# Sharing batch 0's normalisation between two engines, and another order of first loads, in a one-core adaLN block

## The chip, the cores and the metric

The program runs on one core of a Trainium2 chip. The metric is the device time of one execution in microseconds (us). The engines are PE (TensorE, with its weight loads as PEld), DVE (VectorE), ACT (ScalarE), POOL (GpSimd) and SP (SyncE, which here only issues DMAs); "SPq" and "ACTq" are the DMA issues on the queues of SP and ACT.

## What is computed

x is 16 batches of 512 tokens by 128 features, all float32. With h of 128 features:

```python
mod = (silu(c) @ wmod).reshape(16, 6, 1, -1)      # c: [16, 128], wmod: [128, 768]
sa, ca, ga, sb, cb, gb = (mod[:, n] for n in range(6))
ga, gb = sign(g) * max(|g|, 0.25) of each
h = layernorm(x) * (1 + ca) + sa
q = h @ Wq + bq                                    # q, k and v are the same
x = x + ga * (softmax(q @ q.T / sqrt(128)) @ q)    # per batch
h = layernorm(x) * (1 + cb) + sb
# top-1 routing over 8 experts: sigmoid(h @ Wr + br), argmax, its probability as factor
x = x + gb * prob * (gelu(h @ W1[e]) @ W2[e])
```

## The kernel before

A batch is held as a tile of 128 partitions by 4 blocks (j = 0 to 3) of 128 features; a partition holds four consecutive tokens. The kernel has three parts: a head (the modulation from c, and the first batches' start), attention slots (one per batch, each engine with its own hand-written order in which four batches are in work at once), and the expert part (39 tiles of 256 or 128 tokens). In an attention slot k, batch k is scored and mixed, batch k+1 is projected, batch k+2 is normalised, batches k-1 and k-2 are routed. Slots -2 and -1 fill this pipeline.

**The head.** SP issues four loads in this order: `cond` (c, 8 KB, L361), `wmod_sb` (384 KB, L362), x of batch 0 and x of batch 1 (256 KB each, L342). ACT waits for `cond` and computes `cond_e` = exp(-c) (L695), and then issues four small loads on its own queue (Wq, bq, Wr, br; L696 to L699). DVE computes `cond_d`, `cond_s` and `silu` (L879 to L883), then `ln1` of batch 0 (4 statistics L865, 4 aggregates L868) and `variance1` (L874, L875), the copy `silu_t` (L887), and the same of batch 1. POOL turns the variance into `rstd1` by a power (L1376) and then `offset1` (L1379). ACT's `normalize1` writes the four blocks of `xn` (L708).

PE transposes `silu` (L448), and multiplies by `wmod_sb`: four products give shift and scale as columns in the PSUM tile `side[1]` (L452), two give the gate rows in `mixed[1]` (L456). Then `flip_xn` transposes the four blocks of `xn` into `side[1]` (L469). As the columns lie in the same bank, it waits until DVE has copied them out (`s_dve0`, L892 to L895). ACT's `input_t` applies scale and shift and writes `h_t` (L721), PE projects it (`project`, L479), ACT writes `q_t` and `q_hi` (L733, L737), DVE `q_lo` (L919), and PE transposes `q_t` (`flip_v`, L487).

**The gates.** DVE makes `gate_rows` from the two gate products in four instructions (L899 to L904). SP waits for them, stores them to DRAM (L367), waits for the store, and then, in its slots, issues the load of x of batch 2, `load_gate1` of batch 0 (the gate row read back, broadcast to all partitions, L350), x of batch 3, the gate of batch 1, and W1 (2 MB, L375). DVE's `values` needs both the transposes of `flip_v` and this gate:

```python
dve.wait_ge(v_flipped, b.n + 1)
dve.wait_ge(gate1_loaded[b.p], 16 * (b.h + 1))
nc.vector.tensor_tensor(v_sb[:, b.p, :, :], side[1][:]..., gate1[:, b.p, :]..., ALU.mult).then_inc(v_ready, 1)
```

In DVE's order `values` of batch 0 (L928) stands ahead of `find_max` of batch 0, block 0 (L937), whose result the first exponential on ACT needs (L747). In PE's order the scores of batch 0, block 0 (L500 to L502) are followed by `flip_xn` of batch 1, which waits for `v_ready` (the same PSUM bank `side[1]`), and that by the scores of block 1 and `flip_probs` (L512). The later `flip_v`, `values`, `find_max` and `residual` repeat for each batch.

Of the kernel before, what the change touches and what calls it, by code (L numbers as in the profile page):

```python
# [11 lines left out]
ALU = mybir.AluOpType  # L12
# [10 lines left out]
def batch_at(n):  # L23
    return Batch(n, n % 2, n // 2, n % PAYLOADS, n // PAYLOADS, n % X_TILES, n // X_TILES)


def adaln_block(nc, x_in, Wq, bq, Wr, br, W1, W2, c_in, wmod, out):
    B, S, H = x_in.shape
    E, _, F = W1.shape
    J = S // P  # L30
    KF = F // P
# [24 lines left out]
    with ExitStack() as ctx:  # L56
        def sb(name, shape, dt=F32):
            return ctx.enter_context(nc.sbuf_tensor(name, shape, dt))

        def sem(name):  # L60
            return ctx.enter_context(nc.semaphore(name))
# [4 lines left out]
        mixed = [ctx.enter_context(nc.psum_tensor(f"mixed{n}", [P, 512], F32)) for n in range(2)]  # L66
        side = [ctx.enter_context(nc.psum_tensor(f"side{n}", [P, 512], F32)) for n in range(2)]
# [25 lines left out]
        cond = sb("cond", [B, H])  # L93
# [4 lines left out]
        silu_t = sb("silu_t", [P, B])  # L98
        wmod_sb = sb("wmod_sb", [P, 6 * H])
        shift1 = sb("shift1", [P, B])  # L100
        scale1 = sb("scale1", [P, B])
        shift2 = sb("shift2", [P, B])
        scale2 = sb("scale2", [P, B])
# [7 lines left out]
        x_tile = sb("x_tile", [P, X_TILES, J, H])  # L111
# [6 lines left out]
        rstd1 = sb("rstd1", [P, 2, J])  # L118
        rstd2 = sb("rstd2", [P, 2, J])
        neg_mean1 = sb("neg_mean1", [P, 2, J])  # L120
        offset1 = sb("offset1", [P, 2, J])
        xn = sb("xn", [P, J, H])
# [61 lines left out]
        start = sb("start", [1, REST])  # L184
# [26 lines left out]
        cond_loaded = sem("cond_loaded")  # L211
        s_small = sem("s_small")
        s_small2 = sem("s_small2")
        s_dve0 = sem("s_dve0")
# [5 lines left out]
        s_rowsp = sem("s_rowsp")  # L220
# [13 lines left out]
        rstd1_ready = sem("rstd1_ready")  # L234
        offset1_ready = sem("offset1_ready")
        xn_ready = sem("xn_ready")
        xn_flipped = sem("xn_flipped")
        h_ready = sem("h_ready")
        q_projected = sem("q_projected")
# [58 lines left out]
        def wait(eng, s, value):  # L298

            if value > 0:  # L300
                eng.wait_ge(s, value)

        def real(b):
            return 0 <= b.n < B
# [29 lines left out]
        def _(sp):  # L334
            def row(b):
                return slice(b.n, b.n + 1)

            def load_x(b):
                if not real(b):
                    return  # L340
                wait(sp, x1_ready, J * (b.n - X_TILES + 1))
                sp.dma_start(x_tile[:, b.x:b.x + 1, :, :].rearrange("p b j h -> p b (j h)"),  # L342
                             x_view[row(b)].rearrange("b p f -> p b f")
                             ).then_inc(x_loaded[b.x], 16)
# [13 lines left out]
                             gates_dram[row(b), H:2 * H].unsqueeze(1).to_broadcast([P, J, H])  # L358
                             ).then_inc(gate2_loaded[b.q], 16)

            sp.dma_start(cond[:], c_in).then_inc(cond_loaded, 16)  # L361
            sp.dma_start(wmod_sb[:], wmod).then_inc(s_small2, 16)  # L362
            for n in range(2):
                load_x(batch_at(n))

            sp.wait_ge(s_mod, 1)
            sp.dma_start(gates_dram, gate_rows[:]).then_inc(s_mod_dram, 16)  # L367
# [76 lines left out]
        def _(pe):  # L444
# [4 lines left out]
            pe.wait_ge(s_silu_t, 1)  # L449
            pe.wait_ge(s_small2, 16)  # L450
            for n, part in enumerate((0, 1, 3, 4)):
                last = nc.tensor.matmul(side[1][:, n * B:(n + 1) * B], wmod_sb[:, part * H:(part + 1) * H],  # L452
                                        silu_t[:], start=True, stop=True)
            last.then_inc(s_cols, 1)
            for n, part in enumerate((2, 5)):
                last = nc.tensor.matmul(mixed[1][0:B, n * H:(n + 1) * H], silu_t[:],  # L456
                                        wmod_sb[:, part * H:(part + 1) * H], start=True, stop=True)
            last.then_inc(s_rowsp, 1)

            def flip_xn(b):  # L460
                if not real(b):
                    return
                pe.wait_ge(xn_ready, b.n + 1)

                if b.n == 0:
                    pe.wait_ge(s_dve0, 6)
                wait(pe, v_ready, b.n)
                for j in range(J):
                    last = nc.tensor.transpose(side[1][:, j * P:(j + 1) * P], xn[:, j, :], ident[:])  # L469
                last.then_inc(xn_flipped, 1)  # L470

            def project(b):
                if not real(b):
                    return

                pe.wait_ge(h_ready, b.n + 1)
                if b.n == 0:
                    pe.wait_ge(s_small, 64)
                nc.tensor.matmul(side[1][:], wq_sb[:], h_t[:], start=True, stop=True).then_inc(q_projected, 1)  # L479
# [150 lines left out]
            def slot(k):  # L630
                before2, before, now, after, after2 = (batch_at(k + d) for d in range(-2, 3))
                ending = k == B - 1
                score(now, 1)
                flip_probs(now, 0)
                mix(before, 3)
                project(after)
                if ending:
                    flip_rows(0)
                score(now, 2)
                router(before2)  # L640
                flip_probs(now, 1)
                mix(now, 0)
                score(now, 3)
                flip_v(after)
                flip_h2(before2)
                if ending:
                    flip_rows(1)
                flip_probs(now, 2)
                mix(now, 1)
                score(after, 0)  # L650
                flip_probs(now, 3)
                places(before2)
                if ending:
                    up(0)
                mix(now, 2)
                flip_xn(after2)
                flip_xn2(before)
# [33 lines left out]

        @block.scalar
        def _(act):
            act.wait_ge(cond_loaded, 16)
            nc.scalar.activation(cond_e[:], cond[:], ACT.Exp, scale=-1.0).then_inc(s_cond_e, 1)  # L695
            act.dma_start(wq_sb[:], Wq).then_inc(s_small, 16)  # L696
# [4 lines left out]
            def normalize1(b):  # L701
                if not real(b):
                    return
                act.wait_ge(offset1_ready, b.n + 1)
                act.wait_ge(x_loaded[b.x], 16 * (b.xr + 1))
                wait(act, xn_flipped, b.n)
                for j in range(J):
                    last = nc.scalar.activation(xn[:, j, :], x_tile[:, b.x, j, :], ACT.Identity,  # L708
                                                bias=offset1[:, b.p, j:j + 1], scale=rstd1[:, b.p, j:j + 1])
                last.then_inc(xn_ready, 1)  # L710

            def input_t(b):
                if not real(b):
# [145 lines left out]
        def _(dve):  # L859
            def ln1(b):  # L860
                if not real(b):
                    return
                wait(dve, x_loaded[b.x], 16 * (b.xr + 1))
                for j in range(J):
                    nc.vector.bn_stats(stats1[:, b.p, j, :], x_tile[:, b.x, j, :]).then_inc(ln1_stats, 1)  # L865
                for j in range(J):
                    wait(dve, ln1_stats, J * b.n + j + 1)
                    nc.vector.bn_aggr(moments1[:, b.p, j, :], stats1[:, b.p, j, :]).then_inc(ln1_moments, 1)  # L868

            def variance1(b):  # L870
                if not real(b):
                    return
                dve.wait_ge(ln1_moments, J * b.n + J)
                nc.vector.tensor_scalar_mul(neg_mean1[:, b.p, :], moments1[:, b.p, :, 0], -1.0)  # L874
                nc.vector.tensor_scalar_add(var1[:, b.p, :], moments1[:, b.p, :, 1], EPS).then_inc(var1_ready, 1)  # L875
# [10 lines left out]
            dve.wait_ge(s_silu_tp, 1)  # L886
            nc.vector.tensor_copy(silu_t[:], side[0][:, 0:B]).then_inc(s_silu_t, 1)  # L887
            ln1(batch_at(1))
            variance1(batch_at(1))

            dve.wait_ge(s_cols, 1)
            nc.vector.tensor_copy(shift1[:], side[1][:, 0:B]).then_inc(s_dve0, 1)  # L892
            nc.vector.tensor_scalar_add(scale1[:], side[1][:, B:2 * B], 1.0).then_inc(s_dve0, 1)
            nc.vector.tensor_copy(shift2[:], side[1][:, 2 * B:3 * B]).then_inc(s_dve0, 1)
            nc.vector.tensor_scalar_add(scale2[:], side[1][:, 3 * B:4 * B], 1.0).then_inc(s_dve0, 1)  # L895

            dve.wait_ge(s_rowsp, 1)
            g = mixed[1][0:B, 0:2 * H]
# [574 lines left out]
```

## Time and profile before

| | |
|---|---|
| median of 3 runs | 354.69 us (354.61 to 355.04) |
| the profiled execution's own time | 354.34 us |
| its span, first to last instruction | 352.6 us |
| mean granted TensorE clock | 0.986 of full speed |
| PE / DVE / ACT / POOL busy | 92% / 79% / 63% / 55% of the span |

The profile is of one execution. A timeline row gives start, duration, engine, line, operation, output tile and input tiles, how many instructions were merged, and in brackets how long the engine had been idle and what ended that. A row of the chain gives start, length and the piece of work (or transfer) that held up the end; "issue" is time in which nothing visible was waited for. The time of a DMA is from its issue to its landing.

### The profile page before, as it was taken

How to read it: one execution, taken by the hardware profiler on the slowest of the kernel's cores; microseconds unless marked ns; L12 is line 12 of the kernel's file. 1: busy time of each engine (PE TensorE's matmuls, PEld its weight loads, DVE VectorE, ACT ScalarE, POOL GpSimd, SP SyncE). 2: the span in 40 equal slices, each digit the busy share in tenths (PEclk: the TensorE clock that was granted, in tenths of full speed). 3: DMA queues.
4: the chain of work that ended last, by engine and by line, in shares of the span. 5: the costliest groups of instructions: out<-in, count | busy, mean ns of one | idle time of the engine just before them, and what ended most of it. 6: DMA issues, size and time to landing. Idle time of an engine off the chain costs nothing.

```text
span 352.6 us, 8419 instructions
## 1 busy us (share of the span) xinstructions
PE 325.0 (92%) x2578; PEld 299.6 (85%) x2578; DVE 278.9 (79%) x1114; ACT 223.5 (63%) x477; POOL 193.1 (55%) x224
## 2 busy tenths in 40 slices
PE   2799999999999999999989898899999999999960
PEld 2388788889888988898878798899999999999960
DVE  5378898898889888988997896899897777877730
ACT  2589987888788878887866585654445454434320
POOL 5016467545754575457525445877566556565661
PEclk9999999999999999999999999999999999999995
DMA  3394124337653666943536612664989554454300
GB/s 113 116 256 104 44 68 131 100 112 121 146 105 104 123 128 188 249 138 111 105 91 224 231 50 87 186 205 134 289 259 307 166 171 120 127 139 125 93 21 4
DMA packets 34493, 49.27 MB, mean 140 GB/s; under 512 B 4320, under 2 KB 26115, under 8 KB 34448
## 3 DMA queue, kind: packets, MB, share of 16 engines
q1 hardware_dynamic: 27504, 31.74, 37.0%
q0 software_dynamic: 6368, 16.92, 12.9%
q8 instruction: 21, 0.34, 0.4%
q14 instruction: 24, 0.20, 0.2%
q10 hardware_dynamic: 576, 0.07, 0.1%
HBM read 28.21 MB, written 20.96 MB: 139 GB/s over the span
## 4 chain that ended last, share of the span: by engine, by line
PE 70%; DVE 13%; ACT 6%; issue 5%; DVEq 2%; DMA 1%; POOL 1%; POOLq 0%; SPq 0%; ACTq 0%
PE mixed L625 14%; PE mixed L525 12%; PE flipped L512 6%; PE side L479 4%; PE scores L502 3%; PE scores L500 3%; PE scores L501 3%; PE side L545 3%; PE side L469 2%; PE scores L609 2%; PE scores L610 2%; PE scores L608 2%; PE side L537 2%; PE side L487 2%; PE flipped L609 2%
## 5 line engine op out<-in xcount | busy, mean ns | idle before, releaser
L1406 POOL DMA_INDIRECT sorted_rows<-payload,slots x64 | 63.9, 998 | 79.8 <-DVE slots L1044 64.9
L1433 POOL DMA_INDIRECT out_dram<-y_out,tokens x71 | 74.9, 1055 | 42.4 <-DVE y_out L1105 25.8
L625 PE MATMUL mixed<-down_slot,hidden 128*128 128x128 f32 x568 | 70.1, 276 | 2.5 <-ACT hidden L804 2.5
L625 PEld LDWEIGHTS mixed<-down_slot,hidden 128*128 128x128 f32 x568 | 66.5, 192 | 3.0 <-ACT hidden L804 3.0
L525 PE MATMUL mixed<-v_sb,probs_t 128*128 128x128 f32 x512 | 69.0, 278 | 0.0
L747 ACT ACTIVATE probs<-scores,row_max 128x512 f32<-128x512 f32 x64 | 44.0, 687 | 35.1 <-DVE row_max L937 33.4
L525 PEld LDWEIGHTS mixed<-v_sb,probs_t 128*128 128x128 f32 x512 | 62.2, 192 | 0.2
L937 DVE TENSOR_REDUCE row_max<-scores 128x1 f32<-128x512 f32 x64 | 44.1, 688 | 19.0 <-PE scores L502 19.0
L789 ACT ACTIVATE f_hi<-side 128x256 fp32r<-128x256 f32 (+1 forms) x39 | 14.3, 366 | 42.8 <-PE side L587 42.8
L512 PE MATMUL flipped<-ident,probs 128*128 128x128 f32 x256 | 39.1, 275 | 0.4 <-ACT probs L747 0.3
L755 ACT ACTIVATE probs_t<-flipped 128x512 f32<-128x512 f32 x64 | 37.9, 594 | 0.0
L512 PEld LDWEIGHTS flipped<-ident,probs 128*128 128x128 f32 x256 | 31.1, 145 | 5.9 <-ACT probs L747 1.9
L500 PE MATMUL scores<-q_hi,q_lo 128*128 128x512 f32 x64 | 35.7, 557 | 0.0
L1073 DVE CAST up_slot<-w_parts 128x1024 fp32r x39 | 28.0, 719 | 3.2 <-issue 1.4
L708 ACT ACTIVATE xn<-x_tile,offset,rstd 128x128 f32<-128x128 f32 x64 | 26.2, 491 | 5.2 <-POOL offset L1379 5.2
L1376 POOL TENSOR_TENSOR rstd<-var,neg_half 128x4 f32<-128x4 f32 x16 | 19.9, 1243 | 15.7 <-DVE var L875 15.4
L804 ACT ACTIVATE hidden<-flipped 128x512 f32<-128x512 f32 x38 | 22.5, 597 | 7.9 <-PE flipped L610 6.0
L1078 DVE COPY down_slot<-w_sb 128x512 f32 x39 | 17.5, 448 | 11.4 <-PE mixed L625 11.4
L502 PE MATMUL scores<-q_hi 128*128 128x512 f32 x64 | 25.5, 398 | 0.0
L501 PE MATMUL scores<-q_lo,q_hi 128*128 128x512 f32 x64 | 25.3, 396 | 0.0
L1098 DVE SCALAR_TENSOR_TENSOR gated<-mixed,rows 128x128 f32<-128x128 f32 x71 | 21.6, 341 | 3.0 <-PE mixed L625 3.0
L608 PE MATMUL scores<-f_lo,up_slot 128*128 128x256 f32 (+1 forms) x80 | 23.5, 294 | 0.0
(187 smaller groups left out, 768.7 us busy)
## 6 DMA issues: line engine op xcount, KB each, us to landing
rows<-sorted_rows SPq DMA_DIRECT2D x32, 388.0 KB, 3.7
x_tile<-in_L_attn_inputs_dram SPq DMA_DIRECT2D x16, 256.0 KB, 3.2
payload<-stored_gates SPq DMA_DIRECT2D x16, 256.0 KB, 9.3
sorted_rows<-pad_rows SPq DMA_DIRECT2D x9, 388.0 KB, 4.6
w_parts<-in_L_ffn_W_dram SPq DMA_DIRECT2D x1, 2048.0 KB, 8.8
rows<-sorted_rows SPq DMA_DIRECT2D x7, 194.0 KB, 2.6
out_dram<-y_out,tokens POOLq DMA_INDIRECT x71
gate<-stored_gates SPq DMA_DIRECT2D x16, 64.0 KB, 5.8
```

Source lines behind the costliest of these rows:

```text
L500: nc.tensor.matmul(o, q_lo[:, b.p, mine], q_hi[:, b.p, :], start=True, stop=False)
L501: nc.tensor.matmul(o, q_hi[:, b.p, mine], q_lo[:, b.p, :], start=False, stop=False)
L502: nc.tensor.matmul(o, q_hi[:, b.p, mine], q_hi[:, b.p, :], start=False, stop=True).then_inc(scores_ready, 1)
L512: last = nc.tensor.transpose(flipped[j % 2][:, k * P:(k + 1) * P], probs[:, j % 2, k * P:(k + 1) * P], ident[:])
L525: last = nc.tensor.matmul(mixed[j % 2][:, 0:H], probs_t[:, j % 2, k * P:(k + 1) * P], v_sb[:, b.p, k, :], start=(k == 0), stop=(k == J - 1))
L608: nc.tensor.matmul(o, hi, f_lo[:, t % 2, 0:width], start=True, stop=False)
L625: last = nc.tensor.matmul(mixed[t % 2][:, u * H:(u + 1) * H], hidden[:, t % 2, f, u * P:(u + 1) * P], down_slot[:, t % 3, f, :], start=(f ...
L747: nc.scalar.activation(probs[:, j % 2, :], scores[j % 2][:], ACT.Exp, bias=row_max[:, c:c + 1], accum_out=den[:, c:c + 1]).then_inc(exp_do ...
L755: nc.scalar.activation(probs_t[:, j % 2, :], flipped[j % 2][:], ACT.Copy).then_inc(probs_t_ready, 1)
L937: nc.vector.tensor_reduce(row_max[:, c:c + 1], scores[j % 2][:], AX_X, ALU.max, negate=True).then_inc(max_found, 1)
L1406: nc.gpsimd.indirect_dma_start(rows_dram, bass.IndirectOffsetOnAxis(ap=slots[:, c:c + 1], axis=0), payload[:, b.q, j, :], None).then_inc(s ...
L1433: nc.gpsimd.indirect_dma_start(out_rows, bass.IndirectOffsetOnAxis(ap=tokens[:, t % RING, u:u + 1], axis=0), y_out[:, t % RING, u, :], Non ...
```

## The change

SP's first load is now x of batch 0, then wmod, then x of batch 1. `cond` is issued on ACT's queue, as ACT's first instruction. Of batch 0 alone, ACT normalises blocks 0 and 1 and DVE blocks 2 and 3, each block with a count of its own on `xn0_act` or `xn0_dve`, and PE transposes each block when it is there. The shift and scale columns go to the bank `mixed[0]`, so that these transposes no longer wait for the columns to be copied out. The two gate products stand behind batch 0's transposes in PE's order. DVE's two blocks stand between `ln1` and `variance1` of batch 1, and so ahead of the copies of the columns.

```diff
-            sp.dma_start(cond[:], c_in).then_inc(cond_loaded, 16)
+            load_x(batch_at(0))
             sp.dma_start(wmod_sb[:], wmod).then_inc(s_small2, 16)
-            for n in range(2):
-                load_x(batch_at(n))
+            load_x(batch_at(1))
...
             for n, part in enumerate((0, 1, 3, 4)):
-                last = nc.tensor.matmul(side[1][:, n * B:(n + 1) * B], wmod_sb[:, part * H:(part + 1) * H],
+                last = nc.tensor.matmul(mixed[0][:, n * B:(n + 1) * B], wmod_sb[:, part * H:(part + 1) * H],
                                         silu_t[:], start=True, stop=True)
             last.then_inc(s_cols, 1)
-            for n, part in enumerate((2, 5)):
-                last = nc.tensor.matmul(mixed[1][0:B, n * H:(n + 1) * H], silu_t[:],
-                                        wmod_sb[:, part * H:(part + 1) * H], start=True, stop=True)
-            last.then_inc(s_rowsp, 1)
...
-                pe.wait_ge(xn_ready, b.n + 1)
-
-                if b.n == 0:
-                    pe.wait_ge(s_dve0, 6)
+                wait(pe, xn_ready, b.n)
                 wait(pe, v_ready, b.n)
                 for j in range(J):
+                    if b.n == 0:
+                        pe.wait_ge((xn0_act, xn0_dve)[j // 2], j % 2 + 1)
                     last = nc.tensor.transpose(side[1][:, j * P:(j + 1) * P], xn[:, j, :], ident[:])
                 last.then_inc(xn_flipped, 1)
+                if b.n == 0:
+                    gate_products()
+
+            def gate_products():
+                for n, part in enumerate((2, 5)):
+                    last = nc.tensor.matmul(mixed[1][0:B, n * H:(n + 1) * H], silu_t[:],
+                                            wmod_sb[:, part * H:(part + 1) * H], start=True, stop=True)
+                last.then_inc(s_rowsp, 1)
...
+            act.dma_start(cond[:], c_in).then_inc(cond_loaded, 16)
             act.wait_ge(cond_loaded, 16)
...
-                for j in range(J):
+                for j in range(J // 2 if b.n == 0 else J):
                     last = nc.scalar.activation(xn[:, j, :], x_tile[:, b.x, j, :], ACT.Identity,
                                                 bias=offset1[:, b.p, j:j + 1], scale=rstd1[:, b.p, j:j + 1])
-                last.then_inc(xn_ready, 1)
+                    if b.n == 0:
+                        last.then_inc(xn0_act, 1)
+                if b.n > 0:
+                    last.then_inc(xn_ready, 1)
...
             ln1(batch_at(1))
+            dve.wait_ge(offset1_ready, 1)
+            for j in range(J // 2, J):
+                nc.vector.tensor_scalar(xn[:, j, :], x_tile[:, 0, j, :], rstd1[:, 0, j:j + 1], offset1[:, 0, j:j + 1],
+                                        ALU.mult, ALU.add).then_inc(xn0_dve, 1)
             variance1(batch_at(1))
...
-            nc.vector.tensor_copy(shift1[:], side[1][:, 0:B]).then_inc(s_dve0, 1)
+            nc.vector.tensor_copy(shift1[:], mixed[0][:, 0:B]).then_inc(s_dve0, 1)
```

The three other copies of columns change their source in the same way.

## Rows read from the trace of the kernel before

**Rows 1.** The chain of waits in order of time: start, length, what held.
```profile
1.72 3.33 DMA x_tile<-in_L_attn_inputs_dram
...
5.07 0.87 DVE stats L865 x4
...
17.16 0.43 PE scores L502
17.58 0.85 PE side L469 x4
...
18.71 0.23 PE scores L501
```
**Rows 2.** The timeline, first 5 us: loads, the modulation's start.
```profile
0.80 1.28 ACT L695 ACT_TABLE_LOAD   x1 [0.80 <-PEq L1462]
...
0.81 0.40 SPq L361 DMA_DIRECT2D cond<-in_L_c_dram  x1
...
1.26 0.41 SPq L362 DMA_DIRECT2D wmod_sb<-in_L_wmod_dram  x1
...
2.51 0.31 ACT L695 ACTIVATE cond_e<-cond 16x128 f32<-16x128 f32 x1 [0.43 <-DMA cond<-in_L_c_dram]
...
4.34 0.28 DVE L883 TENSOR_TENSOR silu<-cond,cond_s 16x128 f32<-16x128 f32 x1
```
**Rows 3.** DMA issues: size and time from issue to landing, first loads, batch 0's gate.
```profile
cond<-in_L_c_dram SPq DMA_DIRECT2D x1, 8.0 KB, 1.7
wmod_sb<-in_L_wmod_dram SPq DMA_DIRECT2D x1, 384.0 KB, 2.8
...
wr_sb<-in_L_ffn_Wr_dram ACTq DMA_DIRECT2D x1, 4.0 KB, 2.9
x_tile<-in_L_attn_inputs_dram SPq DMA_DIRECT2D x1, 256.0 KB, 2.4
gate<-stored_gates SPq DMA_DIRECT2D x1, 64.0 KB, 3.3
```
**Rows 4.** The timeline, 6 to 12 us: normalisation, products, transposes, gates.
```profile
6.63 1.89 PE L452 MATMUL side<-silu_t,wmod_sb 128*128 128x16 f32 x8 [1.67 <-DVE silu_t L887]
8.01 1.65 ACT L708 ACTIVATE xn<-x_tile,offset,rstd 128x128 f32<-128x128 f32 x4 [5.19 <-POOL offset L1379]
8.45 1.04 PE L456 MATMUL mixed<-wmod_sb,silu_t 128*16 128x128 f32 x4
9.71 1.11 PE L469 MATMUL side<-ident,xn 128*128 128x128 f32 x4 [0.23 <-ACT xn L708]
10.75 0.41 DVE L904 SCALAR_TENSOR_TENSOR gate_rows<-gate_sign,gate_size 16x256 f32<-16x256 f32 x1
10.86 0.78 ACT L721 ACTIVATE h_t<-side,shift,scale 128x512 f32<-128x512 f32 x1 [1.20 <-PE side L469]
```
**Rows 5.** The timeline of VectorE near 38 us: two blocks normalised by `tensor_scalar`.
```profile
37.43 0.60 DVE L980 TENSOR_SCALAR xn<-payload,moments,rstd 128x128 f32<-128x128 f32 x2
```
**Rows 6.** The timeline, 11 to 19 us: projection, gate load, first scores.
```profile
11.69 2.08 PE L479 MATMUL side<-h_t,wq_sb 128*128 128x512 f32 x2 [0.87 <-ACT h_t L721]
...
13.03 0.43 SPq L350 DMA_DIRECT2D gate<-stored_gates  x1
15.22 1.09 PE L487 MATMUL side<-ident,q_t 128*128 128x128 f32 x4 [1.45 <-ACT q_hi L737]
16.39 0.69 DVE L928 TENSOR_TENSOR v_sb<-side,gate 128x512 f32<-128x512 f32 x1 [0.59 <-PE side L487]
17.62 0.69 DVE L937 TENSOR_REDUCE row_max<-scores 128x1 f32<-128x512 f32 x1 [0.54 <-PE scores L502]
```
**Rows 7.** Windows: length; PE, PEld, DVE, ACT, POOL busy; clock, DMA share, GB/s.
```profile
3.00:4.00 1.00, 0.00 (x0) 0.00 (x0) 0.96 (x2) 0.00 (x0) 0.25 (x3) 1.00 0.94 341
15.20:18.40 3.20, 3.18 (x12) 2.77 (x13) 1.98 (x3) 1.45 (x5) 0.00 (x0) 1.00 0.90 289
21.70:28.70 7.00, 7.00 (x55) 6.46 (x54) 4.92 (x14) 6.16 (x16) 1.36 (x2) 1.00 0.80 158
```

More of the change, by code:

```diff
@@ L236, in adaln_block @@
         xn_ready = sem("xn_ready")
+        xn0_act = sem("xn0_act")
+        xn0_dve = sem("xn0_dve")
         xn_flipped = sem("xn_flipped")
@@ L888, in _ @@
             ln1(batch_at(1))
+            dve.wait_ge(offset1_ready, 1)
+            for j in range(J // 2, J):
+                nc.vector.tensor_scalar(xn[:, j, :], x_tile[:, 0, j, :], rstd1[:, 0, j:j + 1], offset1[:, 0, j:j + 1],
+                                        ALU.mult, ALU.add).then_inc(xn0_dve, 1)
             variance1(batch_at(1))
             dve.wait_ge(s_cols, 1)
-            nc.vector.tensor_copy(shift1[:], side[1][:, 0:B]).then_inc(s_dve0, 1)
-            nc.vector.tensor_scalar_add(scale1[:], side[1][:, B:2 * B], 1.0).then_inc(s_dve0, 1)
-            nc.vector.tensor_copy(shift2[:], side[1][:, 2 * B:3 * B]).then_inc(s_dve0, 1)
-            nc.vector.tensor_scalar_add(scale2[:], side[1][:, 3 * B:4 * B], 1.0).then_inc(s_dve0, 1)
+            nc.vector.tensor_copy(shift1[:], mixed[0][:, 0:B]).then_inc(s_dve0, 1)
+            nc.vector.tensor_scalar_add(scale1[:], mixed[0][:, B:2 * B], 1.0).then_inc(s_dve0, 1)
+            nc.vector.tensor_copy(shift2[:], mixed[0][:, 2 * B:3 * B]).then_inc(s_dve0, 1)
+            nc.vector.tensor_scalar_add(scale2[:], mixed[0][:, 3 * B:4 * B], 1.0).then_inc(s_dve0, 1)
             dve.wait_ge(s_rowsp, 1)
```

## The prediction

> **What bounds the kernel now.** The page says PE is busy for 92% of the span, so what counts is how early PE's unbroken work can begin and whether anything delays it. I read the chain of waits first, because the change touches only the first 20 us. It begins with the load of x of batch 0, which lands at 1.72 + 3.33 = 5.05, runs through DVE's statistics, POOL, ACT's normalisation, PE's transposes and the projection, and from 17.58 on stays on PE [rows 1]. In the window from 21.7 to 28.7 PE is busy for all of 7.00 us [rows 7]; whatever shift the engines have at about 19 us is therefore carried to the end, and the question is this shift alone. Second I read the timeline for the head, third the landings of the DMAs, because a side path (gate products, their store, their reload) joins the chain again at `v_sb`.
>
> **Where that side path stands now.** The gate of batch 0 is issued at 13.03 [rows 6] and takes 3.3 us [rows 3]: it lands at 16.33. PE's `flip_v` ends at 15.22 + 1.09 = 16.31 [rows 6]. `v_sb` starts at 16.39, right behind both; the trace names PE, but the gate has no slack against it. `v_sb` ends at 17.08. Behind it DVE idles 0.54 until the scores end at 17.58, and takes the first maximum at 17.62 [rows 6]. So the gate may be 0.54 us later for nothing, and beyond that every microsecond moves the maximum, the first exponential, and PE's first `flip_probs`.
>
> **The change, part by part.**
>
> *x leads SP's queue.* x of batch 0 is issued at 0.81 in place of 1.72. With its old 3.33 it lands at 4.14, with the 2.4 of the shortest x load [rows 3] at 3.2. Either is ahead of DVE, which is busy with the modulation until 4.34 + 0.28 = 4.62 [rows 2]. The statistics thus start at about 4.64 in place of 5.07: 0.43 gained, not 0.91. x of batch 1 is issued 0.46 earlier, and wmod stays second in the queue; wmod landed at 4.06 (2.8 [rows 3] from 1.26 [rows 2]) and is wanted at 6.63 [rows 4] less the shift, so even 1 us later costs nothing.
>
> *cond on ACT's queue.* The 4.62 now depends on it. Issued at 0.80 and landing in the same 1.7 as before [rows 3], it costs nothing; the table load, now behind a DMA issue of 0.4, ends at 1.20 + 1.28 = 2.48, still before 2.51 [rows 2]. But cond no longer goes alone: x starts beside it. Call its delay d. Below it is 0; above, the 4 KB load on ACT's queue under full traffic took 2.9 [rows 3], so d is at most 1.2. I take 0.2, near the lower end, as only one load starts with it, where that row had three large ones in flight. The gain of the front is s = 0.43 - d = 0.23.
>
> *DVE shares the normalisation.* ACT's four blocks took 8.01 to 9.66 at 0.49 each and 0.39 apart [rows 4], so its second ends at 8.89 less s. DVE's two, which start at the same time, cost 0.60 as a pair [rows 5]: 8.02 to 8.62, less s, also in time. They push the column copies back by 0.6, to an end at about 9.4 less s, while `h_t` needs them at 9.8 less s: hidden, with 0.4 to spare. `variance1` of batch 1 is 0.8 later; its result is not wanted before ACT's blocks at about 15. Nothing is charged.
>
> *Transposes per block, no wait for the columns.* PE is busy with the columns until 8.52 less s [rows 4]. Block 0 goes at 8.55, block 1 at 8.93 (ACT's end), blocks 2 and 3 follow 0.23 apart (the four took 1.11, one alone 0.42), and the last ends at 9.80, all less s. Before, it ended at 10.82. So `h_t` comes 1.02 + s = 1.25 earlier.
>
> *Gate products behind them.* They take 1.04 [rows 4]: 9.73 to 10.77 less s. `h_t` ends at 9.84 + 0.78 = 10.62 less s, so the projection waits at most 0.1 for them, starts near 10.70 less s (was 11.69), and PE's main path gains 1.0 + s = 1.2. But the gate products ended at 9.49 before, so the gate path is later by 10.77 - 9.49 - s = 1.28 - s = 1.05. Nothing on it has slack: DVE's four gate instructions, the store, x of batch 2 and the gate's load follow one another on DVE and SP. bq_root, behind them on DVE, moves to 12.4 and is wanted by `q_hi` at about 13: hidden. The loads of x 2, x 3 and W1 move by the same 1.05. The first of them stands right ahead of the gate in SP's order and takes 2.4 [rows 3], so it lands before the gate does, and DVE wants it only behind the first two maxima: hidden.
>
> **The sum.** The gate lands at 16.33 + 1.05 = 17.38. `v_sb` runs 17.44 to 18.13. PE has by then finished the first scores (17.58 - 1.2 = 16.4) and stands before batch 1's transposes, which wait for `v_sb`. The first maximum starts at 18.13 in place of 17.62: +1.05 - 0.54 = **+0.51 us**. The exponential and `flip_probs` follow it one for one. PE fills the time between with batch 1's transposes and the second scores, which take half of 0.85 and three times 0.23 at the fast pace [rows 1], 1.1 in all from 18.13, and so end at 19.3; the maximum and the exponential, 0.69 each or a little more, end behind 19.5. The wait removed on one path is paid on the other. The profiled execution had 354.34 with a span of 352.6 and would have 354.85 and 353.1; the median shown is 0.35 above the profiled one, so on it the forecast is 354.69 + 0.51 = **355.2 us**.
>
> Bounds of this case: d of 0 gives +0.31. If the gate's load took the 2.4 of an x load [rows 3] in place of 3.3 the shift is -0.39 (354.3); it is a broadcast behind an x load in both kernels, so I keep 3.3. With d near 0.4 the shift reaches +0.71. Its own range is 354.7 to 355.5.
>
> **The rivals.** What a measurement of this kernel tells from no change is about 0.2%, 0.7 us.
>
> *A. cond is held up by x.* Both go to the same DMA engines at the same moment. If x's 256 KB move first at the 341 GB/s of the window from 3 to 4 us [rows 7], cond comes 0.77 later, s is -0.34, and the shift is 0.31 + 0.77 = +1.08: 355.8, slower. For it: the small loads on ACT's queue under traffic took 2.9. Against: at 0.80 nothing is in flight yet, and cond has 8 KB. It decides from d = 0.4. The Trainium skill (DMA: Bandwidth & Descriptors, Queues, rings and completion order) states that each DMA engine takes turns between queues a whole packet at a time, and that a completion count lands only after every earlier write of that engine, whatever its queue; by that rule this rival is more than a guess, and the 2.9 agrees with it.
>
> *B. The gate does not bind.* The waits name PE's transposes, not the gate, as what `v_sb` waited for. If the gate really is there with the quickness of the smallest load (1.7 [rows 3]), at 15.8, most of the main path's 1.0 + s = 1.2 comes through: 353.5, faster. Below a load of 2.8 us the shift is already negative. Against: the load's landing at 16.33 is measured, and `v_sb` starts 0.08 after PE's end, twice the 0.04 between PE's scores and the maximum.
>
> *C. PE's pace rises later.* The granted clock reads 1.00 in the whole head [rows 7], yet a 128x512 score product takes 0.43 at 17.16 and 0.23 at 18.71 [rows 1]: half rate (1.2 GHz) first, full rate (2.4 GHz) from about 18.5, after PE had been busy 3.18 of 3.20 us [rows 7]. Now PE stands idle from 16.4 to 18.1. If it then works a further 3.3 us at half rate, half of that is lost, less the 0.4 that batch 1's transposes already paid: 1.65 - 0.4 on top of 0.51 is +1.8, 356.5. Against: PE now works without a pause from 6.4 to 12.6, where before it had gaps at 9.5 and 10.8, so the pace may be up long before. That alone gains nothing, as the gate is waited for; only if it rose before 9.5 would the gate products shrink by half, 0.5, and the shift be zero. The Trainium skill (TensorE: Matmul & The Clock Gate, What's actually happening) says that the slow rate is the resting state and sustained work releases it; the trace agrees in the pace of the products and not in the clock column.
>
> **How the numbers follow.** Forecast (v_sb waits for the gate, d up to 0.4): 0.47. A: 0.2. C: 0.08. B: 0.1. A gate load well under 3.3 or quicker gate products, 354.1 to 354.7: 0.15. The range 354.0 to 356.3 leaves out B, C and a small tail of A and of the last case. Faster by over 0.7 us: B and a little of the last, 0.14. Slower: A, C and the upper edge of the forecast, 0.34. Within: 0.52.
>
> **What would show it.** Statistics start at 4.8 (4.6 if cond is undisturbed, over 5 if A). `h_t` starts at 9.6. `gate_rows` ends at 12.2 in place of 11.16, and the gate is issued at 14.1. `v_sb` starts near 17.4, with about 2 us of idle DVE before it, named to the gate's DMA; the first maximum follows with no gap; PE shows a gap of 1.7 us before batch 1's transposes. B would show `v_sb` at 15.2 and the maximum at 16.4; C would show 0.43 per score product after 18.5. The forecast is wrong if the gate's load takes another time behind the x load than it did, or if the stretch after 19 us does not carry the shift one for one.

## The result, and the profile after

The changed kernel takes 356.02 us (median of 12 runs, 355.46 to 356.83), the kernel before beside it 354.88 (12 runs, 354.39 to 355.69): a ratio of 1.0035, 95% interval 1.0024 to 1.0046. That is 1.1 us slower by the medians, 0.35% by the ratio. Ratios here and below compare the fast executions of either kernel alone, so they can differ from the ratio of the two medians. The profiled execution has a span of 354.2 us (before: 352.6).

The timeline of the changed kernel's head, in the same columns as [rows 2], [rows 4] and [rows 6]:

```profile
0.80 0.42 ACTq L698 DMA_DIRECT2D cond<-in_L_c_dram  x1
0.81 0.40 SPq L344 DMA_DIRECT2D x_tile<-in_L_attn_inputs_dram  x1
...
3.22 0.31 ACT L700 ACTIVATE cond_e<-cond 16x128 f32<-16x128 f32 x1 [0.69 <-DMA cond<-in_L_c_dram]
...
4.79 0.28 DVE L891 TENSOR_TENSOR silu<-cond,cond_s 16x128 f32<-16x128 f32 x1
5.00 0.85 DVE L873 BATCH_NORM_STATS2 stats<-x_tile 128x6 f32<-128x128 f32 x4
...
7.92 0.88 ACT L713 ACTIVATE xn<-x_tile,offset,rstd 128x128 f32<-128x128 f32 x2 [4.39 <-POOL offset L1391]
7.92 0.60 DVE L899 TENSOR_SCALAR xn<-x_tile,rstd,offset 128x128 f32<-128x128 f32 x2 [0.38 <-POOL offset L1391]
...
9.68 1.04 PE L472 MATMUL mixed<-wmod_sb,silu_t 128*16 128x128 f32 x4
9.79 0.78 ACT L729 ACTIVATE h_t<-side,shift,scale 128x512 f32<-128x512 f32 x1 [0.99 <-PE side L465]
...
10.65 1.72 PE L483 MATMUL side<-h_t,wq_sb 128*128 128x512 f32 x2
...
11.98 0.41 DVE L916 SCALAR_TENSOR_TENSOR gate_rows<-gate_sign,gate_size 16x256 f32<-16x256 f32 x1
...
13.81 0.63 PE L491 MATMUL side<-ident,q_t 128*128 128x128 f32 x4 [1.45 <-ACT q_hi L745]
...
14.30 0.43 SPq L352 DMA_DIRECT2D gate<-stored_gates  x1
...
17.66 0.69 DVE L940 TENSOR_TENSOR v_sb<-side,gate 128x512 f32<-128x512 f32 x1 [3.26 <-DMA gate<-stored_gates]
18.26 0.68 DVE L949 TENSOR_REDUCE row_max<-scores 128x1 f32<-128x512 f32 x1
...
18.49 0.90 PE L465 MATMUL side<-ident,xn 128*128 128x128 f32 x4 [3.07 <-DVE v_sb L940]
...
20.71 0.69 DVE L949 TENSOR_REDUCE row_max<-scores 128x1 f32<-128x512 f32 x1 [1.77 <-PE scores L506]
...
56.09 1.02 PE L483 MATMUL side<-h_t,wq_sb 128*128 128x512 f32 x2
```

The main path did what the change says: `h_t` starts at 9.79 (10.86 before), and the transposes of `q_t` at 13.81 (15.22). Then DVE, ACT and PE all wait. `v_sb` waits 3.26 us, and the releaser is now the gate's DMA. It starts 1.27 us later than before, the first maximum 0.64 later (18.26 for 17.62 in [rows 6]), and PE stands idle for 3.07 us. The other 0.63 us were to spare: before, the maximum started 1.23 us behind `v_sb`'s start, here 0.60.

The chain of waits, which in [rows 1] led from x over the statistics and `xn`, now leads from cond over the gate:

```profile
0.80 2.40 DMA cond<-in_L_c_dram
...
10.76 0.41 DVE gate_sign L911
...
12.42 1.47 DMA stored_gates<-gate_rows
...
14.30 3.26 DMA gate<-stored_gates
17.66 0.70 DVE v_sb L940
18.49 0.90 PE side L465 x4
19.39 0.43 PE scores L504
19.82 0.43 PE scores L505
20.25 0.43 PE scores L506
20.67 0.85 PE flipped L516 x4
21.53 1.22 PE side L483 x2
22.74 0.23 PE scores L504
```

The score products from 19.39 to 20.67 take 0.43 each, from the start of one to the start of the next; before, they took 0.23 from 18.71 on [rows 1]. (The timeline counts a product to its own end and so gives 0.63 and 0.40.) Windows of the changed kernel (columns as in [rows 7]) put a number to it:

```profile
15.40:18.50 3.10, 0.03 (x2) 0.04 (x1) 0.84 (x2) 0.00 (x0) 0.00 (x0) 1.00 0.68 221
18.50:21.60 3.10, 3.10 (x12) 2.70 (x13) 1.33 (x4) 1.61 (x4) 0.00 (x0) 0.53 0.86 279
21.60:24.80 3.20, 3.20 (x18) 2.28 (x18) 2.39 (x12) 2.95 (x6) 1.21 (x2) 0.92 1.05 401
```

PE was busy for 0.03 us of 15.4 to 18.5, and its granted clock in the next 3.1 us was 0.53, nearly all at the lower of its two levels (1.2 GHz). So the late gate is paid twice: 0.64 us as a wait, and again as half pace behind it. The second maximum, which PE's scores release in both kernels, starts at 20.71 in place of 19.21, 1.50 later. The row before, and that of the second mark used below:

```profile
19.21 0.69 DVE L937 TENSOR_REDUCE row_max<-scores 128x1 f32<-128x512 f32 x1 [0.89 <-PE scores L502]
...
54.33 1.02 PE L479 MATMUL side<-h_t,wq_sb 128*128 128x512 f32 x2
```

To follow both, I use two marks in every trace: the start of the first maximum (`row_max` of batch 0, block 0), and the start of the projection of batch 4 (its PE row out of `h_t`, `wq_sb`), which lies where the rhythm of 11.8 us a batch has set in. They stand at 17.62 and 54.33 before, and at 18.26 (+0.64) and 56.09 (+1.76) after. What the second mark loses beyond the first is lost between them, and before the projection of batch 2, at about 30 us: from the projection of batch 2 to that of batch 4 every trace of this document takes 24.5 us. The second mark foretells the end. The spans of the profiled executions on chips where the times are steady differ from the 352.6 before by +1.6 (changed kernel, mark +1.76), +3.7 (before_gates_behind, +3.65) and -0.7 (gates_lead_2, -0.90).

### The profile page after: what moved, and what is told of

It is laid out like the page before. It is cut to its first block, busy times and chain, and to the rows that moved or that the text cites. A ratio compares the mean times of both kernels' runs of the same rounds, so it can differ in the third digit from the quotient of the medians.

```text
span 354.2 us, 8418 instructions
## 1 busy us (share of the span) xinstructions
PE 324.9 (92%) x2578; PEld 299.7 (85%) x2578; DVE 279.6 (79%) x1116; ACT 222.6 (63%) x475; POOL 192.3 (54%) x224
## 4 chain that ended last, share of the span: by engine, by line
PE 68%; DVE 15%; ACT 5%; issue 5%; DMA 2%; DVEq 2%; POOLq 0%; POOL 0%; SPq 0%; ACTq 0%
PE mixed L629 14%; PE mixed L529 12%; PE flipped L516 6%; PE scores L506 3%; PE scores L504 3%; PE scores L505 3%; PE side L483 3%; PE side L549 3%; PE side L465 2%; PE scores L613 2%; PE scores L614 2%; PE scores L612 2%; PE side L541 2%; PE flipped L613 2%; PE flipped L614 2%
## 5 line engine op out<-in xcount | busy, mean ns | idle before, releaser
L1090 DVE COPY down_slot<-w_sb 128x512 f32 x39 | 18.9, 485 | 11.8 <-PE mixed L629 11.8
```

## The experiments

Nine of the twelve runs fell on chips where the kernel before itself had medians of 369 to 375 us and scattered over 6 to 12 us from run to run (a scattering chip, below); their times decide little. Their first 60 us look as on the other chips, so there the two marks decide. before_gates_behind, before_no_gate0 and gates_lead_2 ran on a quiet chip, where the kernel before took 354.57.

### cond back on SP's queue (cond_sp)

```diff
-            act.dma_start(cond[:], c_in).then_inc(cond_loaded, 16)
+            sp.dma_start(cond[:], c_in).then_inc(cond_loaded, 16)   # ahead of load_x(batch_at(0))
```

> Theory 1 (the changed kernel loses twice: the gate's load lands 1.27 us later, which moves the first maximum from 17.62 to 18.26, and PE then falls back to half pace because it idled for 3.1 us): cond lands after 1.7 us again in place of 2.4, the gate path is 0.3 to 0.4 us earlier, the first maximum starts at 17.9 to 18.0, and PE still idles for about 3 us and works at half pace behind it. Against before +0.6 to +0.9 us by the median, so about 355.6. Rival (the late cond is the whole loss): back at before or faster, 354.9 or less.

The changed kernel but for cond. The first maximum starts at 17.70 (+0.08 against before; I had expected 17.9 to 18.0) and the projection of batch 4 at 56.24 (+1.91). The time was 1.4% over before by the ratio (1.0086 to 1.0198), with medians of 376.37 against 374.68, on a chip that scatters. The timeline, from gate to second scores:

```profile
2.36 0.31 ACT L700 ACTIVATE cond_e<-cond 16x128 f32<-16x128 f32 x1 [0.28 <-DMA cond<-in_L_c_dram]
...
4.34 0.28 DVE L891 TENSOR_TENSOR silu<-cond,cond_s 16x128 f32<-16x128 f32 x1
...
17.09 0.69 DVE L940 TENSOR_TENSOR v_sb<-side,gate 128x512 f32<-128x512 f32 x1 [2.79 <-DMA gate<-stored_gates]
17.70 0.68 DVE L949 TENSOR_REDUCE row_max<-scores 128x1 f32<-128x512 f32 x1
...
17.93 1.09 PE L466 MATMUL side<-ident,xn 128*128 128x128 f32 x4 [2.60 <-DVE v_sb L940]
...
20.94 1.91 PE L484 MATMUL side<-h_t,wq_sb 128*128 128x512 f32 x2
```

This is the clearest separation in the case. The wait itself is gone (0.08 us), and nearly all the loss is still there: PE idled for 2.60 us, and 1.83 us went between the marks, where even the projection of batch 1 took 1.91 at half pace (1.12 is what the same row takes before). The rival, that the late cond is the whole loss, falls.

Here the fall of the clock can be dated, too (windows, columns as in [rows 7]):

```profile
15.90:16.00 0.10, 0.00 (x0) 0.00 (x0) 0.00 (x0) 0.00 (x0) 0.00 (x0) 0.85 0.65 77
16.00:16.10 0.10, 0.00 (x0) 0.00 (x0) 0.00 (x0) 0.00 (x0) 0.00 (x0) 0.50 0.27 92
```

PE had worked from 13.72 to 15.33, behind 1.45 us of idling, and its clock fell at about 15.98, only 0.65 us after its last product; it was up again at 22.8. In the changed kernel PE had worked from 13.81 to 15.43, behind 1.45 us of idling as well, but the clock fell only at 18.7, 0.2 us after PE had begun to work again; it was up at 22.1. So nearly the same work ahead of a gap did not make the fall come at the same moment.

### Gate products ahead of the transposes again (gates_first, gates_first_2)

```diff
+            gate_products()
...
                 last.then_inc(xn_flipped, 1)
-                if b.n == 0:
-                    gate_products()
```

The first line stands right behind the four column products.

> The gate products stand ahead of batch 0's transposes again; all else as changed. Theory 1: they end at about 9.4, the gate lands near 16.3, v_sb ends at 17.0, the first maximum starts at about 17.0 (-0.6 against before), and PE idles only about 1 us before batch 1's transposes. Median 354.0 to 354.6, faster than before. Rival (the gate path has nothing to do with it; shared normalisation or the queue of loads costs): stays near 356.

> The kernel with the gate products ahead of the transposes again, as the times of its first run scattered over 5 us. By its trace the projection of batch 4 started at 53.96, 0.37 earlier than in the kernel before; so 0.2 to 0.6 us faster than before by the median, and 1.4 or more faster than the changed kernel. Rival (only the profile of one execution showed that): same as the changed kernel.

The first maximum starts at 17.15 and 17.25 (-0.47, -0.37), the projection of batch 4 at 53.96 and 54.04 (-0.37, -0.29), both earlier than in the kernel before, where the changed kernel is later by 0.64 and 1.76. The normalisation is shared as in the changed kernel, the order of loads and the late cond are the same: none of these is the culprit. By time, on scattering chips, the ratios to before were 1.0048 (0.9998 to 1.0097) and 0.9994 (0.9939 to 1.005), which leave both a small gain and a small loss open.

### Batch 0's values without the read-back gate (no_gate0, before_no_gate0)

```diff
+                if b.n == 0:
+                    nc.vector.tensor_tensor(v_sb[:, 0, :, :], side[1][:]..., unit[:], ALU.mult).then_inc(v_ready, 1)
+                    return
                 dve.wait_ge(gate1_loaded[b.p], 16 * (b.h + 1))
```

`unit` is a tile of ones made by POOL; SP waits for the old gate load before it overwrites its tile for batch 2.

> Batch 0's values are multiplied by a tile of ones that is ready long before, not by the gate that was read back, so batch 0's output lacks its gate and nothing waits for that load. Theory 1: v_sb starts right behind the transposes at 14.5, the first maximum at about 15.5, PE never idles over 1.5 us and keeps the full pace: 2.0 to 2.6 us less than before, about 352.6. Rival (DMA or DVE contention costs the time): within 0.7 us of the changed kernel's 356.0.

> The kernel before, with batch 0's values multiplied by a tile of ones that is ready long before (batch 0's output lacks its gate). It shows what the gate cost in the kernel before. Theory 1 (it had 0.54 us to spare against the first scores): v_sb starts within 0.1 of 16.35, the first maximum at 17.6, the projection of batch 4 at 54.3, and the time is that of the kernel before. Rival (the gate already bound): v_sb and what follows over 0.3 us earlier.

In the changed kernel, `v_sb` starts at 15.32, released by PE's transposes, the first maximum at 16.60, the projection of batch 4 at 53.31: -1.02 at both marks. The main path's gain, which I had put at 1.0 + s = 1.2, is real: 1.02, with an s of 0.1 (below), shows once nothing waits for the gate. My number for this run, 2.0 to 2.6, was wrong: it started from the fast transposes of the profiled execution (0.63 at 13.81), and here they were slow (1.09). The time was 0.983 of before by the ratio (0.974 to 0.993), with medians of 371.00 against 374.68, on a scattering chip: its size can't be read from that.

In the kernel before, the same edit changes nothing: `v_sb` at 16.34, first maximum at 17.62, batch 4 at 54.32, time ratio 0.9994 (0.9982 to 1.0005) on a quiet chip. So the kernel before did not lose time to its gate. What it had to spare was small: DVE's idle 0.54 us ahead of `row_max`, and 0.09 more, as a DVE instruction that follows at once starts 0.60 us behind `v_sb`'s start and not 0.69.

### The one part alone (before_gates_behind)

```diff
-            for n, part in enumerate((2, 5)):                # the two gate products
...
                 last.then_inc(xn_flipped, 1)
+                if b.n == 0:
+                    for n, part in enumerate((2, 5)):        # the same, behind batch 0's transposes
```

This is the kernel before with nothing else of the change.

> The kernel before with one part of the change alone: the two gate products stand behind batch 0's transposes. Theory 1 (this part makes the loss): they end at about 11.8 in place of 9.49, the gate lands about 2.3 us later, at 18.6, v_sb ends at 19.4, the first maximum starts 1.8 us later than 17.62, and the projection of batch 4 starts 1.8 to 2.9 us later than 54.33, the more the longer PE works at half pace behind its idling. Rival (the loss is in the new order of loads or in DVE's share): the projection of batch 4 within 0.3 us of 54.33.

357.98 us against 354.57 on a quiet chip, ratio 1.0095 (1.0079 to 1.0112): this part alone costs 3.4 us. Its timeline:

```profile
13.01 0.41 DVE L904 SCALAR_TENSOR_TENSOR gate_rows<-gate_sign,gate_size 16x256 f32<-16x256 f32 x1
...
15.30 0.43 SPq L350 DMA_DIRECT2D gate<-stored_gates  x1
...
18.53 0.69 DVE L928 TENSOR_TENSOR v_sb<-side,gate 128x512 f32<-128x512 f32 x1 [2.74 <-DMA gate<-stored_gates]
19.13 0.68 DVE L937 TENSOR_REDUCE row_max<-scores 128x1 f32<-128x512 f32 x1
...
21.10 0.63 PE L502 MATMUL scores<-q_hi 128*128 128x512 f32 x1
...
22.38 1.91 PE L479 MATMUL side<-h_t,wq_sb 128*128 128x512 f32 x2
```

The first mark has +1.51 (expected +1.8), the second is at 57.98, +3.65, beyond the 1.8 to 2.9 that I had expected. The wait comes as the sum foresees: the gate is issued 2.27 later, `v_sb` starts 2.14 later, and 0.63 of that was to spare. Between the marks 2.14 us more are lost. There PE works without a gap, and its products keep the length of the lower level until 25 us. In this execution PE had not reached its full pace ahead of the gap, which was only 1.79 us long.

### Work in PE's gap (filler, filler14, filler10)

```diff
+                if b.n == 1:
+                    for n in range(24):                      # 14 and 10 in the two others
+                        nc.tensor.transpose(flipped[1][:, 0:P], ident[:], ident[:])
                 wait(pe, v_ready, b.n)
```

> 24 transposes of the identity into a free PSUM bank fill PE's idle time behind the first scores, nothing else is changed. Theory 1: the full pace holds through the wait, batch 1's transposes take 0.5 us in place of 0.90, second scores 0.23 each, and of the 1.8 us by which the trace was late at 23 us only 0.65 is left: 1.0 to 1.2 us less than the changed kernel, about 355.0 to 355.4. Rival (the pace does not matter, since exponentials set the time there): same as the changed kernel, 356.0.

> 14 in place of 24 transposes of the identity behind the first scores (the 24 took until 19.4, longer than the gate needs). Theory 1: they end before v_sb does, batch 1's transposes start near 18.4 and run at full pace, the projection of batch 4 starts at about 55.0, 1.1 us before the changed kernel's. Rival (half pace does no harm): 56.1 as in the changed kernel.

> The changed kernel with 10 transposes of the identity behind the first scores; they take at most 2.3 us at half pace and so end by the time v_sb does, which 14 and 24 did not. Nothing of the gate's path moves. Theory 1 (about half of the loss is PE's pace after its idling): batch 1's transposes and the second scores run at full pace more often, and the median is 0.4 to 1.0 us under the changed kernel's, 355.0 to 355.6, or +0.4 to +0.9 against before. Rival (the pace plays no part in the loss): +1.1 to +1.3 against before, as the changed kernel.

| | fillers | batch 1's transposes | first maximum | batch 4 |
|---|---|---|---|---|
| changed kernel | none | 18.49 | 18.26 (+0.64) | 56.09 (+1.76) |
| filler | 16.25 to 19.56 | 19.39 | 17.95 (+0.33) | 55.32 (+0.99) |
| filler14 | 16.14 to 19.33 | 19.12 | 18.13 (+0.51) | 55.48 (+1.15) |
| filler10 | 15.66 to 16.96 | 18.55 | 18.42 (+0.80) | 55.11 (+0.78) |

The 24 and the 14 overstayed: batch 1's transposes started 1.35 and 0.91 us behind the end of `v_sb`. Nevertheless the second mark came 0.77 and 0.61 earlier than without them, of which 0.31 and 0.13 are the first mark's. filler14 missed what I had expected: the transposes took 1.02, at half pace, and batch 4 came at 55.48 and not at 55.0. The 10 did what they were meant to. PE's timeline:

```profile
15.66 1.30 PE L465 MATMUL flipped<-ident 128*128 128x128 f32 x10
18.55 0.66 PE L470 MATMUL side<-ident,xn 128*128 128x128 f32 x4 [1.59 <-DVE v_sb L945]
18.97 0.47 PE L509 MATMUL scores<-q_hi,q_lo 128*128 128x512 f32 x1
19.28 0.39 PE L510 MATMUL scores<-q_lo,q_hi 128*128 128x512 f32 x1
```

The chain of waits no longer runs over these transposes and scores:

```profile
18.50 0.61 DVE row_max L954
...
19.96 0.66 PE flipped L521 x4
```

The gap shrank from 3.07 to 1.59 us, the transposes behind it took 0.66 in place of 0.90 and the products 0.39 in place of 0.63 (timeline), and the two marks lose the same: +0.80 and +0.78. With the pace kept, PE's work fits into the time of the first maximum and its exponential, and the gate's wait is all that is left, in this one trace. The times scatter too much to say so: 1.0021 of before (0.998 to 1.0062) for filler10, 0.9971 (0.9913 to 1.0028) for filler14, a median of 372.44 against 374.68 for filler.

### The changed kernel again (after_2)

> The changed kernel itself once more, as a control beside the three others. Theory 1 (late gate, then half pace on PE behind 3 us of idling): v_sb waits for the gate's DMA until about 17.6, a 128x512 score product behind it takes 0.43, and the projection of batch 4 starts at about 56.1 (before: 54.33). If the pace is high there by chance, the projection of batch 4 starts near 55.0. Against before +1.1 us by the median.

First maximum at 18.27, batch 4 at 55.78 (+1.45), ratio 1.0073 (1.0019 to 1.0128) on a scattering chip. The gate's part repeats to 0.01 us; the pace's part does not: in this execution the transposes of `q_t` took 1.09 where they took 0.63 above, so PE had not reached its full pace before the gap, idled for 1.95 us, and reached it at about 21.

### Gate products first of all (gates_lead, gates_lead_2)

```diff
+            for n, part in enumerate((2, 5)): ...            # gate products, then s_rowsp
+            columns(0)                                       # shift1, scale1 into mixed[0]
...
                 last.then_inc(xn_flipped, 1)
                 if b.n == 0:
-                    gate_products()
+                    columns(2)                               # shift2, scale2 into scores[1]
```

DVE follows this order: gate_sign, its two blocks of `xn`, the two first columns, the three other gate instructions, `variance1`, the other columns. cond leads SP's queue. ACT's `h_t` waits for the first two columns, and the router's input for the others.

> cond leads SP's queue; PE does the gate products first of all, then the columns of batch 0's first norm, its transposes, and the other columns behind them; DVE interleaves the gate instructions with its two blocks. Theory 1: gate_rows ends at about 9.7 in place of 12.4, the gate lands at about 15.0, in time for v_sb at 15.3, h_t still starts at 9.4 to 9.8, and PE has no gap over 1.5 us. The first maximum starts at 16.0 to 16.6, 1.0 to 1.6 before the kernel before; the projection of batch 4 at 52.8 to 53.3. Median 353.5 to 353.9. Rival (the head's gains are lost again before the steady part): same as before, 354.9.

> The kernel with the gate products first once more, for its time. By its first trace: gate_rows ends at 9.6, the first maximum starts at 16.1, the projection of batch 4 at 52.8, 1.5 us before the kernel before. If the rest of the program carries that one for one: 1.2 to 1.6 us faster by the median. Rival (lost again later): within 0.3 us of the kernel before.

Its second run was on a quiet chip: 353.02 us against 354.57, ratio 0.9954 (0.9939 to 0.997), that is 1.5 us faster than the kernel before, and with the 1.1 of the result an estimated 2.7 faster than the changed kernel. The first had 1.0018 (0.9964 to 1.0072) on a scattering one. The timeline of the second run:

```profile
9.18 0.41 DVE L915 SCALAR_TENSOR_TENSOR gate_rows<-gate_sign,gate_size 16x256 f32<-16x256 f32 x1
10.17 2.08 PE L486 MATMUL side<-h_t,wq_sb 128*128 128x512 f32 x2 [0.20 <-ACT h_t L731]
...
15.01 0.69 DVE L943 TENSOR_TENSOR v_sb<-side,gate 128x512 f32<-128x512 f32 x1 [0.73 <-DMA gate<-stored_gates]
16.10 0.69 DVE L952 TENSOR_REDUCE row_max<-scores 128x1 f32<-128x512 f32 x1 [0.40 <-PE scores L509]
```

`gate_rows` ends at 9.59, 2.8 us before the changed kernel's and 1.6 before the old one's; the projection starts at 10.17, no later than the 10.20 of cond_sp, which has the same loads. The first maximum starts at 16.10 and 16.09 (-1.5) in the two runs, released by PE's scores, and batch 4 at 52.79 and 53.43 (-1.54, -0.90). The difference of the two runs lies again in the pace: the second scores took 0.23 each in the first run and 0.43 in the second. These runs change the order on PE and on DVE and put cond back on SP's queue all at once; what each part is worth was not tried.

## Why the prediction was right, and where it was short

The measured 356.02 lies in the range (354.0 to 356.3), above the forecast of 355.2 and above the forecast case's own range (354.7 to 355.5). It was slower by more than 0.2%, to which I had given 0.34, less than to no change (0.52). The kernel before measured 354.88 beside it, 0.19 above the 354.69 from which the sum starts. That the time lies in the range is in part luck. The range reached so far up for rival A, whose +1.08 did not come; what filled that room was rival C, which the range was meant to leave out, in a milder form than its price. By its steps:

- **The gate path and its lack of spare time: right.** `v_sb` waits for the gate, its row names it, and before_no_gate0 shows that nothing was lost to it before. The spare time was 0.63, not 0.54, and the shift of the first maximum was +0.64 for +0.51 forecast. The gate was issued at 14.30 (forecast 14.1) and took 3.3 again.
- **Front of the chain, s = 0.23: mis-sized.** cond took 2.4 on ACT's queue in place of 1.7, so d was 0.7, not 0.2: rival A's condition, with the 0.77 that was computed for it. But DVE lost only 0.45 of it. `silu` ended at 5.07 for 4.62, as `cond_d` took 0.21 in place of 0.48 (below). The statistics began at 5.00 (5.07 before), the column products at 6.54 (6.63), so s was about 0.1 and not A's -0.34. The 0.43 itself was too small: in cond_sp, with cond undisturbed, the column products begin at 6.09, 0.54 earlier.
- **Shared normalisation and transposes per block: right.** DVE's pair took 0.60 as read from [rows 5]; the last transpose ended at 9.76 where the sum had 9.80 less s; `h_t` gained 1.07 (forecast 1.25; the difference is s).
- **Gate products behind the transposes, 1.28 - s later: right in kind.** They ended at 10.72 against 9.49, +1.23; the sum had +1.05, and most of the difference is s. The main path's 1.0 + s was real too (no_gate0, -1.02).
- **PE's pace: the step that was wrong.** The sum said that PE's transposes and second scores run at the fast pace, take 1.1 us in all and end inside the exponential's time. They took 2.2 us, from 18.49 to 20.67, and set the chain. Rival C, which says so, had a chance of 0.08. The reason I gave against C, that PE's unbroken work from 6.4 to 12.6 may bring the full pace early, did happen in the profiled execution (the transposes of `q_t` took 0.63), and did not help. It ended the first scores at 15.43 (16.4 in the sum) and so made the gap 3.07 us long, not 1.7; behind it the granted clock was 0.53 for 3.1 us. C's price, 1.3 beyond the gate's, lies inside what the traces lose between the two marks (1.1 in the changed kernel, 0.8 in after_2, 1.8 in cond_sp, 2.1 in before_gates_behind): all four traces with a late gate and nothing in the gap show the loss, so a chance of 0.08 was too small. cond_sp, with the wait gone and the pace lost, shows the pace as a cause of its own, and filler10, with the pace kept and the wait left, shows the other half.

By the median the total was +1.14, less than the +1.76 of the profiled execution's second mark. As the moment of the pace's rise differs between executions of one kernel (in before too, perhaps), how much of the 1.14 is wait and how much pace is known for the traced executions only.

## What to carry to other kernels

When work is moved behind the critical path, follow what it feeds to its end: here two small products fed a store, a reload and a multiplication with 0.63 us to spare in front of everything, and moving them alone cost 3.4 us. Count a new gap on TensorE twice, as the wait and as the half pace behind it, above all in the head of a kernel, where gaps of 1.8 to 3.1 us in these traces were followed by 2.5 to 5.6 us at the lower level. A gap of 1.59 us behind filler work at full pace cost no pace. A side path with two DMA round trips belongs early in every queue that it passes: with the gate products first of all and cond back on SP's queue, both paths gained and the kernel became 1.5 us faster than before.

## What the runs showed of the hardware

- A load of 8 KB that took 1.5 to 1.7 us ahead of everything on SP's queue took 2.2 to 2.4 on ACT's queue (8 traces), beside a load of 256 KB issued 0.01 us later on SP's.
- DVE's `cond_d`, 16x128, took 0.48 when it started at 2.85, 0.63 at 2.70, 0.62 at 2.71 (it ended at 3.33 each time), and 0.21 at 3.56. POOL runs its constants meanwhile, the last from 3.10 to 3.26. In before_no_gate0, where one more memset moved POOL's constants 0.46 later, it took 0.28 from 2.84. That its length goes with what POOL does fits these rows, but was not tested, nor which instruction of POOL it would be. It made the first part of cond's delay free (0.7 later at ACT, 0.45 at `silu`).
- The granted clock reads 1.00 for a kernel's first products although their durations are those of the lower level (0.43 for a 128x512 score product against 0.23); it shows the lower level only after a first fall (0.53 from 18.50 to 21.60). In after_2 and before_gates_behind, where the pace had not risen ahead of the gap, it reads 1.00 behind the gap too, beside products of 0.43. The pace in the head has to be read from durations.
- The same program reached the full pace before its gap in one execution (transposes of `q_t` 0.63) and not in another (1.09).
- A full pace was lost 0.65 us after PE's last product in cond_sp and 3.3 us after it in the changed kernel, with 1.6 us of work behind 1.45 of idling ahead of both.
